# Four-layer transformer on one core: the first two attention layers score each head twice, by query and by key

## The reference, cut to what matters

```
S = q k^T                      # 256 x 256, float32
S = S - 10000 where key > query      # layer 0 only (causal)
P = exp(S - max over keys) ; out = (P v) / sum over keys of P
```

## Time and profile before

| | us |
|---|---|
| median of three runs | 3285.16 |
| profiled execution | 3288.66 |
| its span | 3287.4 |
| first scores of `attention8` | 51.34 |
| block 16 (layer 1) begins | 390.58 |
| block 29 begins | 650.78 |
| first matmul behind `attention8` | 716.47 |
| PE / DVE / ACT / POOL busy in the span | 93% / 81% / 74% / 61% |

### The profile page before, as it was taken

The page is one execution under the profiler, slowest core; times in us unless marked ns, Lnnn a source line. Parts: engine busy times, 40 slices in busy tenths (PEclk is TensorE's granted clock), DMA queues, the critical chain, the costliest instruction groups (busy, mean ns, idle before and its releaser), DMA issues.

```text
span 3287.4 us, 75219 instructions
## 1 busy us (share of the span) xinstructions
PE 3049.8 (93%) x25143; PEld 2380.6 (72%) x25143; DVE 2669.5 (81%) x6092; ACT 2430.9 (74%) x6888; POOL 1995.5 (61%) x1981
## 2 busy tenths in 40 slices
PE   6999999998699998999989999999999999999997
PEld 5777777766588878788777777777777777777775
DVE  7999999976877776365458888888888888888886
ACT  7888888874355556536438888888888888888885
POOL 3432323322255545515318888888888888888884
PEclk9999999999799998999989999999999999999998
DMA  3222422200000000200100000000000000000000
GB/s 116 64 64 66 128 79 84 78 21 7 1 1 1 1 29 21 69 16 20 43 13 2 2 1 2 2 2 2 1 2 2 2 2 2 2 2 2 2 2 27
DMA packets 67147, 80.49 MB, mean 24 GB/s; under 512 B 7696, under 2 KB 57936, under 8 KB 66512
## 3 DMA queue, kind: packets, MB, share of 16 engines
q1 hardware_dynamic: 65472, 75.27, 7.4%
q10 hardware_dynamic: 1296, 0.41, 0.1%
HBM read 56.79 MB, written 18.87 MB: 23 GB/s over the span
## 4 chain that ended last, share of the span: by engine, by line
PE 37%; DVE 9%; POOL 8%; issue 5%; ACT 3%; DVEq 0%; POOLq 0%; ACTq 0%
PE psum L2507 9%; PE psum L2489 7%; PE psum L2471 6%; POOL attn_p L2969 4%; DVE attn_pt L2768 2%; DVE sb_few L2755 2%; PE psum L1853 2%; PE psum L1704 2%; PE psum L1946 2%; ACT attn_p L2613 2%; PE psum L1706 2%; PE psum L1705 2%; PE psum L1753 2%; PE psum L2534 1%; PE psum L2413 1%
## 5 line engine op out<-in xcount | busy, mean ns | idle before, releaser
L2969 POOL TENSOR_TENSOR attn_p<-attn_p,sb_few 128x512 f32<-128x512 f32 x768 | 796.0, 1050 | 174.9 <-DVE sb_few L2762 173.8
L2613 ACT ACTIVATE attn_p<-psum,sb_few 128x256 f32<-128x256 f32 x1536 | 720.2, 479 | 61.1 <-DVE sb_few L2755 61.0
L2755 DVE TENSOR_REDUCE sb_few<-psum 128x2 f32<-128x512 f32 x768 | 508.0, 679 | 12.1 <-PE psum L2471 6.7
L2489 PE MATMUL psum<-sb_kept,attn_p 128*128 128x128 f32 x3072 | 412.4, 277 | 32.9 <-DVE attn_pt L2768 29.2
L537 ACT ACTIVATE sb_a_p<-psum,sb_a_nm 128x256 f32<-128x256 f32 x1024 | 406.9, 500 | 11.2 <-DVE sb_a_nm L464 11.1
L2507 PE MATMUL psum<-attn_pt,attn_v 128*64 128x256 f32 x3072 | 385.0, 387 | 30.4 <-DVE attn_pt L2768 30.4
L2489 PEld LDWEIGHTS psum<-sb_kept,attn_p 128*128 128x128 f32 x3072 | 336.0, 141 | 82.4 <-issue 30.5
L464 DVE TENSOR_REDUCE sb_a_nm<-psum 128x2 f32<-128x512 f32 x512 | 328.3, 683 | 39.6 <-PE psum L358 25.5
L2613 ACT ACTIVATION_READ_ACCUMULATOR attn_p<-psum,sb_few 128x1 f32 x1536 | 319.6, 208 | 0.0
L2507 PEld LDWEIGHTS psum<-attn_pt,attn_v 128*64 128x64 f32 x3072 | 203.0, 136 | 157.3 <-issue 76.3
L588 POOL TENSOR_TENSOR sb_a_rot<-sb_a_t 128x256 f32<-128x256 f32 x64 | 46.6, 728 | 430.3 <-DVE sb_a_t L444 430.2
(11 more groups left out here) (436 smaller groups left out, 8011.9 us busy)
## 6 DMA issues: line engine op xcount, KB each, us to landing
sb_a_spread<-a_spilled SPq DMA_DIRECT2D x96, 256.0 KB, 3.0
a_spilled<-sb_a_part_hi SPq DMA_DIRECT2D x64, 128.0 KB
a_spilled<-sb_a_part_lo SPq DMA_DIRECT2D x64, 128.0 KB
sb_a_spread<-a_spilled SPq DMA_DIRECT2D x32, 128.0 KB, 2.7
sb_gate_up<-in_L_ffn_Wg SPq DMA_DIRECT2D x32, 128.0 KB
sb_gate_up<-in_L_ffn_Wu SPq DMA_DIRECT2D x32, 128.0 KB
sb_down_w<-in_L_ffn_Wd SPq DMA_DIRECT2D x32, 128.0 KB, 2.6
sb_x<-in_L_attn_x SPq DMA_DIRECT2D x4, 512.0 KB, 7.4
```

Source lines behind the costliest of these rows:

```text
L2489: mm = pe.transpose(PT(e)[:, kt * N + t * P:kt * N + (t + 1) * P], Pr[p % 3][:, e, t, kt * P:(kt + 1) * P], c.ident)
L2613: ins = act.activation(Pr[p % 3][:, e, t, :], S(p, e)[:, t * N:(t + 1) * N], ACT.Exp, bias=nm[:, p % 4, e, t:t + 1], accum_out=rsum[:, p % ...
L2755: dve.tensor_reduce(nm[:, p % 4, e, :], S(p, e).rearrange("p (t n) -> p t n", t=TB), AX.X, ALU.max, negate=True).then_inc(maxed.sem, 1)
L2969: pool.tensor_tensor(P3, P3, spread(rinv[:, p % 4, e, :], N), ALU.mult).then_inc(normed[e].sem, 1)
```

## The change

Scores are computed twice. `scores` as before serves the maxima alone and runs 13 steps ahead (AHEAD = 8 + 5). When a block's 16 heads have their maxima, POOL splits them into hi and lo (`part_maxima`), PE transposes the 64 columns (`turn_maxima`, at j = 3), ACT copies them and issues two transfers from its own queue that write them as rows into spare partitions of the q tile (`lay_maxima`), where k's tile has ones. `scores_by_key` then computes key by query, with the maximum already subtracted, ACT takes a plain exponential of 512 columns straight into the tile that `weigh` reads, and the transposes, `move_even` and `move_odd` are gone. In layer 0 the mask is added on both sides (`hide`, `hide_by_key`).

The scores take three banks of PSUM in turn, those by key three others, so `scores` waits for a maximum of the step before, and `scores_by_key` for an exponential of the step before. `weigh`, `turn_back` and `settle` come two steps earlier. The tiles of q and k are three deep instead of two; `project` and `rope_turn` run three blocks ahead instead of two. POOL's order becomes: lay q, lay k of b, part q of b+1, part_maxima of b-1, part k of b+1. `lay` of block b waits for the end of block b-3's `scores_by_key`. The expert weights are issued in four portions behind blocks 16 to 19. In layer 1 the spread's second transfer is half as large as before.

The core of the diff:

```diff
+    S = lambda p, e: c.banks[(2 * p + e) % 3]
+    ST = lambda p, e: c.banks[3 + (2 * p + e) % 3]
+    AHEAD = PB + 5
+        def scores_by_key(p):
+            if j == 0:
+                pe.wait_ge(*maxima_laid(32 * (b + 1) - 1))
+            if p:
+                pe.wait_ge(*exped(2 * p - 2))
+            for t in range(TB):
+                for e in range(2):
+                    mm = pe.matmul(ST(p, e)[:, t * N:(t + 1) * N], ks[b % 3][rows_of(h), h // 4, t * P:(t + 1) * P],
+                                   q[b % 3][rows_of(h), h // 4, :], start=(t == 0 or not causal), stop=not causal,
...
-        for p in range(NP + 7):
+        for p in range(-AHEAD, NP + 7):
             b, j = divmod(p, PB)
+            ahead = p + AHEAD
+            if 0 <= p < NP:
+                scores_by_key(p)
+            if ahead < NP:
+                scores(ahead)
+            if 0 <= p < NP and layer(b)[3]:
+                hide_by_key(p)
+            if ahead < NP and layer(ahead // PB)[3]:
+                hide(ahead)
+            if j in (0, 2) and -1 <= b and b + 3 < NB8:
+                project(b + 3, j // 2)
...
+            act.activation(PTs[p % 4][:, e, :, :], ST(p, e).rearrange("p (k n) -> p k n", k=TB), ACT.Exp).then_inc(exped.sem, 1)
+        def lay_maxima(b):
+            act.wait_ge(*maxima_turned(b))
+            act.copy(nm_rows[:, :], M[0:2 * H8 * TB, 0:P]).then_inc(maxima_copied.sem, 1)
...
+            for n in range(2):
+                act.dma_start(dst, nm_rows[n * half:(n + 1) * half, :]).then_inc(maxima_laid.sem, 16)
...
-            if b >= 2:
-                pool.wait_ge(*scored((b - 1) * PB - 1))
-            pool.tensor_copy((q, ks)[j][b % 2][:, :, :], spreads[j][:, :, :]).then_inc(laid.sem, 1)
+            if b >= 3:
+                pool.wait_ge(*scored_keys((b - 2) * PB - 1))
+            pool.tensor_copy((q, ks)[j][b % 3][:, :, :], spreads[j][:, :, :]).then_inc(laid.sem, 1)
...
-        for b in range(1, NB8):
+        for b in range(1, NB8 + 1):
+            if b < NB8:
+                for j in range(2):
+                    lay(b, j)
             if b + 1 < NB8:
-                for j in range(2):
-                    part(b + 1, j)
...
+                part(b + 1, 0)
+            part_maxima(b - 1)
+            if b + 1 < NB8:
+                part(b + 1, 1)
```

More of the change, by code:

```diff
@@ L353, in scores @@
                                    skip_group_check=causal)
-            if causal:
-                for e in range(2):
-                    for t in range(TB):
-                        mm = pe.matmul(S(p, e)[:, t * (N + P):t * (N + P) + P], c.mask400, c.future, start=False, stop=True,
-                                       skip_group_check=True)
-            mm.then_inc(scored.sem, 1)
[L362 to L366, removed]
+            if not causal:
+                mm.then_inc(scored.sem, 1)
@@ L367, in turn, with hide, hide_by_key @@
+        def hide(p):
+            for e in range(2):
+                for t in range(TB):
+                    mm = pe.matmul(S(p, e)[:, t * (N + P):t * (N + P) + P], c.mask400, c.future, start=False, stop=True,
+                                   skip_group_check=True)
+            mm.then_inc(scored.sem, 1)
+        def hide_by_key(p):
+            for e in range(2):
                 for t in range(TB):
-                    mm = pe.transpose(PT(e)[:, kt * N + t * P:kt * N + (t + 1) * P],
-                                      Pr[:, p % 3, e, t, kt * P:(kt + 1) * P], c.ident)
@@ L507, in dve_program @@
                 make_masks()
-        for p in range(NP + 8):
+        for p in range(-AHEAD, NP + 8):
             b, j = divmod(p, PB)
-            if p % 2 == 0 and 6 <= p < NP + 6:
-                settle((p - 6) // 2)
-            if j == 7 and b:
+            ahead = p + AHEAD
+            if p % 2 == 0 and 4 <= p < NP + 4:
+                settle((p - 4) // 2)
+            if j == 7 and b >= 1:
                 add(b - 1)
[L514 to L519, removed]
+            if ahead < NP:
+                maxima(ahead, 0)
+                maxima(ahead, 1)
             if 2 <= b < B + 2 and j == 2:
                 between.statistics(b - 2)
-            if j in (0, 2) and b + 2 < NB8:
-                rope_turn(b + 2, j // 2)
-            elif j == 4 and b + 1 < NB8:
+            if j in (0, 2) and -1 <= b and b + 3 < NB8:
+                rope_turn(b + 3, j // 2)
+            elif j == 4 and 0 <= b and b + 1 < NB8:
                 lay_v(b + 1, 0)
@@ L560, in act_program @@
             beside.act_step(j + beside.first)
[L561 removed]
+        for p in range(-AHEAD, NP + 7):
             b, j = divmod(p, PB)
[L563 removed]
+            if j == 6 and b >= 1:
                 copy_out(b - 1)
[L565 to L566 removed]
+            if p % 2 and 3 <= p < NP + 3:
+                copy_sums((p - 3) // 2)
             if j == 2 and 3 <= b < B + 3:
@@ L638, in sp_program @@
                     sp.wait_ge(*laid(2 * (b - 1) + j))
+                if b == B and j == 0:
+                    for g in range(GQ):
+                        dst = bass.AP(tensor=spreads[0], offset=11 * wide + g * N, ap=[[ROW * wide, 4], [1, N]])
+                        sp.dma_start(dst, c.const("early")[0, :].partition_broadcast(4)).then_inc(masks.sem, 16)
                 for n in range(2):
-                    if n and layer(b)[3]:
+                    if n:
                         src = bass.AP(tensor=box, offset=wide * (1 - j), ap=[[2 * wide, ROW], [1, wide]])
```

202 lines of the change are left out of this document (112 added, 90 removed).

## The result

| | before | changed |
|---|---|---|
| median (lowest to highest), us | 3283.9 (3282.6 to 3290.0) | 3226.2 (3224.3 to 3231.3) |
| profiled execution (span), us | 3288.66 (3287.4) | 3228.11 (3226.8) |
| first scores; end of the stage, us | 51.34; 716.47 | 52.86; 660.19 |
| stages behind it, us | 2570.9 | 2566.6 |

The medians are of four executions each. The changed kernel takes 0.9818 of the time (95% interval 0.9806 to 0.9831), 1.8% or about 60 us less. Forecast were 3242 us in a range of 3215 to 3272.

What follows compares the result with a forecast made beforehand. PE was taken to bound the kernel. Layer 0's gain was to pay for the start, then layer 1's relay at 18.0 us a block would end the stage 43 us sooner: 3242 us, range 3215 to 3272.

Steps and rivals of the forecast that it cites:

- The relay becomes the loop of layer 1: POOL and SP's relay of q and k, closed by POOL's order, sets layer 1's pace: 18.0 us a block.
- rival 1: Layer 1: the relay doesn't bind, PE keeps 16.4 us a block, 24 us more gain, 3218 us; chance 0.20.
- Scores by key at 0.43 us a step: PE, each step: scores by key cost 0.43 us like the scores; layer 0's block takes 19.85 us.
- The start: First thirteen steps of scores alone, each bound by its maximum: 24.7 us, between 19.5 and 28; first scores by key at 76.
- The expert portions: Layer 1's relay: expert weights, issued in fourths, add 2 us to each of three turns.
- Behind the last laid k: End of the stage: PE's remaining blocks 29 to 31 and the tail take 40 us, ending at 673.4.
- The clock in layer 1: PE's clock falls to 0.93 in layer 1; PE asks 17.6 us, under 18.0, so no effect and no chance given.
- all of layer 0's gain pays for the start: Layer 0's shorter blocks only make up for the start: block 16 begins at 390.6 us, as before.
- Rival 2: Layer 1: the relay is slower, some 19.5 us a block, 14 x 1.5 us lost, 3263 us; chance 0.22.
- rival 3: Both layers: the relay takes 21 us a block, 60 us lost, 3302 us, slower than before; chance 0.08.

Runs made afterwards that it cites:

- Opening the ring: Changed kernel with POOL splitting the next block's q before it lays this block's k: 3202.94 us, ratio 0.9736 to the kernel before.
- the ring open, six banks and the loads moved: Changed kernel with POOL's next q split before laying k, six score banks for the first 13 steps, expert weights behind blocks 2 to 13: 3182.38 us.

## Why the prediction was right, and where it was not

By its steps, all from the changed kernel's trace:

- **The relay becomes the loop of layer 1: right, in mechanism and size.** 18.0 us were forecast, 17.9 measured. The legs were 4.8 for q's spill (4.4 forecast), 5.1 for k's (5.4), 3.7 for k's spread (3.8), 2.0 from laid k to q's spill. PE stands at j = 3, as was said, for the split of q and of the maxima, up to 1.9 us a turn (2 forecast). Opening the ring gave 27 us, the 24 of rival 1 and a little more; rival 1's 3218 us is near the changed kernel's time, but its reason is false: the relay does bind.
- **Scores by key at 0.43 us a step: the failed term.** I took "less they can hardly cost" from the number and columns of the matmuls, and never asked whether they run behind the others or beside them. They add 0.01 us to the scores' 0.43, in odd steps as seen and in even ones as far as the wait for the maximum lets one see: 8 x 0.42 = 3.4 us a block less than forecast. But the block is 18.2 instead of 19.85, only 1.65 less, because waits came out that this work was to cover. I had put them at 0.3 a block. `scores` waiting for the maximum of the step before were to stand 0.12 at most, behind 0.43 of scores by key; with these running beside, an even step pays 0.27 (0.71 for eight instead of 0.44), 1.1 a block. Scores by key waited for exponentials of the step before, 6.4 us between 89 and 360 us, 0.4 a block (228.16 shows one, 0.33), a loop that I had put inside the step; ACT's exponential takes 597 ns, as I took it from the earlier trace rows, and it is the shorter PE step that lets it show. That gives 19.85 − 3.4 − 0.3 + 1.1 + 0.4 = 17.65 of the measured 18.2; 0.1 more is idle time before L349, the remaining 0.4 or so I can't place. From the first scores by key to the start of block 16 it is 294.4 us (81.44 to 375.79) instead of 314.6: −20.2.
- **The start: inside its bounds, at the wrong end.** 28 us was my figure for a clock of 1.2 GHz throughout, and I took 24.7. The clock was 0.50 for all of it, the steps 2.12: 28.6 from first scores to first scores by key. The first scores themselves came 1.5 later, which I had not counted; in the seven further runs, with the same opening, they came at 51.6 to 53.6, so it is at least in part the spread of executions. In sum +5.4. The row to trust was the one of the very stretch, 0.53 at 83% busy: the change makes PE less busy there, not more.
- **The expert portions:** 19.1, 20.2 and 19.1 us for their turns against 17.9, in sum 4.8; 6 were forecast.
- **Behind the last laid k:** 43.3 us (laid at 616.9, end of the stage at 660.19) against 40.
- **The clock in layer 1:** 0.91, where I had 0.93. It made no term, as said, since PE had slack under the ring; a `weigh` took up to 1.94 us instead of 1.07 in those stretches.

The sum: +5.4 (start) − 20.2 (layer 0) − 1.7 (from the start of block 16 to the last laid k) + 3.3 (end) = −13.2, the difference of 673.4 and 660.19. That "all of layer 0's gain pays for the start" was thus false: block 16 begins near 376 us instead of 390.58. That the sum lies only 13 us off is in part luck: the overlap alone was worth twice what layer 0 shows, and waits that I had nearly left out, and a slow start, took the other half back.

On the overlap a rule of the Trainium skill could have been weighed (TensorE: Matmul & The Clock Gate, Part 3: Packing small matmuls — row/col tiling): matmuls of 32 rows that lie on different row groups run at the same time. The trace agrees in odd steps (0.44 us for eight, 0.43 for four), and in even ones the wait for the maximum stands in front of it. Had I applied it, the term would have been near zero and PE's own block of layer 0 19.85 − 8 x 0.43 = 16.4 us; then the relay's 18.0 would have set layer 0's pace too. That is close to the measured 18.2, but for a reason that is false: with the ring open layer 0 kept 18.3, so PE and its waits set it.

Rival 2 (a relay of 19.5) and rival 3 (21) were wrong: q's spill took 0.4 us more than forecast, k's 0.3 less, and the turn 17.9.

## What to carry to other kernels

Before pricing an added group of matmuls by its number and columns, look at what stands next to it and at which rows of PE each uses: here two groups on different rows cost as much as one, on the same rows 1.6 times as much, and with other work between them twice as much, and the distance between two loops decided which rows met. Then ask which waits the added work was to cover: where it costs nothing, it covers nothing. When a change reorders an engine that takes part in a relay of transfers, write the relay down as a ring: if its last step stands ahead of the next turn's first on one engine, its length is the pace, and swapping these two is the first thing to try. And when one engine's load falls, look for transfers that sit in the stage that is now bound by latency, and move them to the one that isn't.

## What the runs showed of the hardware

- Eight matmuls of 32 rows and 256 columns: 0.86 us apart from each other, 0.68 side by side on the same rows, 0.44 on different rows. Where eight on different rows took longer, 0.58 to 0.76 in even steps, the second four had to wait for DVE's maximum and started 0.06 us behind its end.
- Four bf16 mask matmuls on 128 rows took 0.23 us with other matmuls on 128 rows behind them (239.77 to 240.00) and 0.33 with 32-row scores behind them (239.01 to 239.34).
- The granted clock in layer 1 was 1.00 before, with PE at 99%, 0.91 in the changed kernel, 0.96 with the ring open alone, and 0.99 with the ring open, six banks and the loads moved. With one more step of lead it was 0.56 and 0.50 (1.2 GHz) over stretches of 20 us in which PE was hardly idle for 0.1 us. There the price isn't hidden any more: blocks went up to 25.7 us.
- A spill, two transfers of 128 KB from SBUF to HBM, took 4.8 and 5.1 us from the first issue to the end of SP's wait (511.52 to 516.32, 517.63 to 522.75); over twelve turns of layer 1 q's took 4.8 to 5.4 and k's 5.0 to 5.6.
